# Two folded attentions: the softmax's maximum goes into ScalarE's bias and its sum comes from ScalarE's accumulator

## The reference, cut to what matters

```
h = (x - mean) / sqrt(var + 1e-5)
scores[b, head, s, k] = (h Wq) . (ctx Wk) * 64 ** -0.5      # 32 keys k; a mask, all true
x = x + softmax(scores over k) (ctx Wv) Wo
```

## Time and profile before

| | |
|---|---|
| median of 3 runs | 574.77 us (573.92 to 574.93) |
| profiled execution | 573.43 us, of which the span from the first to the last instruction is 571.6 us |
| TensorE busy | 483.7 us (85%), mean granted clock 0.901 |
| VectorE busy | 325.1 us (57%) |
| ScalarE busy | 238.7 us (42%) |
| GpSimd busy | 241.6 us (42%) |

### The profile page before, as it was taken

How to read it: one execution, slowest core, us unless ns; L and a number is a source line. 1 busy time by engine, 2 the same in 40 slices (tenths; PEclk the granted TensorE clock), 3 DMA queues, 4 the chain that set the end, 5 groups by cost and what they waited for, 6 DMA issues and landing times.

```text
span 571.6 us, 9125 instructions
## 1 busy us (share of the span) xinstructions
PE 483.7 (85%) x3256; PEld 388.0 (68%) x3256; DVE 325.1 (57%) x1137; ACT 238.7 (42%) x473; POOL 241.6 (42%) x350
## 2 busy tenths in 40 slices
PE   2799894779869986995495599999899899999997
PEld 2558383769556625683385399998553788899997
DVE  4866427844996832778751155643776944433334
ACT  2653744324246541444650054421644395334340
POOL 5781866455326011277777525663760340000000
PEclk9799997559758997996599699999999999999999
DMA  9999720311860056800111212114500000000002
GB/s 275 334 205 208 216 99 1 110 34 36 274 193 1 1 147 162 245 1 0 34 51 50 79 57 81 45 34 157 149 2 0 2 2 0 1 1 1 1 1 75
DMA packets 56861, 48.04 MB, mean 84 GB/s; under 512 B 6082, under 2 KB 47240, under 8 KB 56688
## 3 DMA queue, kind: packets, MB, share of 16 engines
q1 hardware_dynamic: 53728, 42.06, 26.5%
q0 software_dynamic: 2656, 4.88, 2.7%
q10 hardware_dynamic: 432, 0.52, 0.4%
HBM read 35.21 MB, written 12.82 MB: 84 GB/s over the span
## 4 chain that ended last, share of the span: by engine, by line
PE 61%; DVE 23%; POOL 6%; issue 5%; ACT 2%; DMA 1%; ACTq 0%; POOLq 0%; DVEq 0%
PE ps L1266 10%; PE ps L1204 7%; DVE st L1660 5%; PE ps L1087 4%; PE ps L1089 4%; PE ps L1088 4%; POOL tok L2381 4%; PE ps L835 3%; PE ps L775 3%; PE ps L722 2%; PE ps L765 2%; DVE mv L1663 2%; PE ps L858 2%; PE ps L838 2%; DVE mx L1698 2%
## 5 line engine op out<-in xcount | busy, mean ns | idle before, releaser
L2113 DVE SCALAR_TENSOR_TENSOR x<-ps,gate,x 128x128 f32<-128x128 f32 x128 | 36.0, 344 | 54.8 <-PE ps L1266 54.8
L1266 PEld LDWEIGHTS ps<-moe_w,big 128*128 128x128 f32 x512 | 61.1, 192 | 3.9 <-issue 1.7
L1538 ACT ACTIVATE big<-ps,col 128x512 f32<-128x512 f32 x64 | 42.2, 689 | 48.2 <-PE ps L1089 48.1
L1266 PE MATMUL ps<-moe_w,big 128*128 128x128 f32 x512 | 61.4, 275 | 0.9 <-DVE x L2102 0.9
L2472 POOL DMA_INDIRECT res<-qT,dest x43 | 42.5, 988 | 40.7 <-DVE qT L2088 25.6
L722 PE MATMUL ps<-con,xn 128*128 128x128 f32 x148 | 28.6, 326 | 28.8 <-ACT xn L1474 15.4
L1530 ACT ACTIVATE big<-ps 128x320 f32<-128x320 f32 x56 | 24.0, 439 | 56.7 <-PE ps L1089 56.6
L722 PEld LDWEIGHTS ps<-con,xn 128*128 128x128 f32 x148 | 19.8, 167 | 39.2 <-DVE xn L1678 35.8
L1204 PE MATMUL ps<-moe_w,big 128*128 128x128 f32 x344 | 41.1, 275 | 0.6 <-ACT big L1530 0.6
L2271 POOL TENSOR_SCALAR rstd<-mv 128x4 f32<-128x4 f32 (+1 forms) x35 | 9.0, 258 | 76.8 <-DVE mv L1663 75.8
L1204 PEld LDWEIGHTS ps<-moe_w,big 128*128 128x128 f32 x344 | 39.8, 192 | 0.8 <-ACT big L1530 0.8
(11 more groups left out here) (353 smaller groups left out, 1179.7 us busy)
## 6 DMA issues: line engine op xcount, KB each, us to landing
ring<-in_ew SPq DMA_DIRECT2D x20, 256.0 KB, 4.8
moe_w<-in_m0w SPq DMA_DIRECT2D x16, 256.0 KB, 6.3
moe_w<-in_m2w SPq DMA_DIRECT2D x16, 256.0 KB, 5.6
tok<-zero SPq DMA_DIRECT2D x1, 2580.0 KB, 27.6
big<-tok SPq DMA_DIRECT2D x7, 322.5 KB, 2.9
res<-zero SPq DMA_DIRECT2D x1, 2048.0 KB, 29.1
moe_w<-in_ew SPq DMA_DIRECT2D x8, 256.0 KB, 5.6
big<-res SPq DMA_DIRECT2D x4, 512.0 KB, 5.0
```

The source lines that it names most:

```text
L1266: last = mm(ps[7 - i % 2 if i >= B else 6 + i % 2][:, cols(c)], big[:, FC * (e % 2) + f, i % B, cols(c)], w[:, e, F + P * f:F + P * f + P] ...
L1538: A(big[:, 2 * (e % 2) + f, t, :], bank[:, :], ACT.Gelu, bias=V("m3b1", 2 * e + f)).then_inc(h_act, 1)
L2113: last = v.scalar_tensor_tensor(out=x[:, C * t + c, :], in0=bank[:, cols(c)], scalar=gate[:, C * t + c, e:e + 1], in1=x[:, C * t + c, :], ...
```

## The change

VectorE no longer subtracts the maximum and no longer sums. It turns each maximum m into -m * rstd with a scalar_tensor_tensor on the maxima alone (in L1 two of these, since its chunks lie in another order than rstd's), and waits for rstd before it. ScalarE's exponential takes this as its bias, exp(rstd * s + (-m * rstd)), and gives the sum over the keys from its accumulator. Bias and sum belong to one head of one chunk, so there is now one exponential per chunk and head: 8 of 128x32 for an L1 tile instead of 4 of 128x64, and 4 of 128x32 for an L2 tile as before. The mask's constant BIG becomes a power of two.

```diff
-BIG = 1e30
+BIG = 2.0 ** 100
...
             def fsoft(name):
-                smax, norm, R = n["smax"], n["norm"], ATT[name]["R"]
+                smax, norm, H = n["smax"], n["norm"], ATT[name]["H"]
 
                 def stage(t):
                     act.wait_ge(s_max[t], smax)
                     act.wait_ge(rstd_ready[t], rstds(t, norm))
                     for q in range(C):
                         c = C * t + chunk_at(name, q)
-                        mine = big[:, 0, t, R * q:R * (q + 1)]
-                        last = A(mine, mine, ACT.Exp, scale=rstd[:, c:c + 1])
+                        for h in range(H):
+                            mine = soft(name, t)[:, q, h, :]
+                            last = A(mine, mine, ACT.Exp, bias=mx[:, C * t + q, h:h + 1], scale=rstd[:, c:c + 1],
+                                     accum_out=rs[:, C * t + q, h:h + 1])
                     last.then_inc(f_exp, 1)
...
             def fscore(name):
                     link(v.tensor_tensor(soft(name, t), s_, mask, ALU.add))
                     link(v.tensor_reduce(top, soft(name, t), AX.X, ALU.max))
-                    v.tensor_tensor(soft(name, t), soft(name, t), bc(top, [P, C, H, NK], [3]), ALU.subtract).then_inc(s_max[t], 1)
+                    dve.wait_ge(rstd_ready[t], rstds(t, norm))
+                    apart = 2 if name == "L1" else 1
+                    for a in range(apart):
+                        m = C // apart
+                        i = v.scalar_tensor_tensor(out=top[:, m * a:m * a + m, :], in0=top[:, m * a:m * a + m, :], scalar=-1.0,
+                                                   in1=bc(rstd[:, C * t + a:C * t + C:apart], [P, m, H], [2]), op0=ALU.mult, op1=ALU.mult)
+                    i.then_inc(s_max[t], 1)
...
             def fsoft(name):
                     total = rs[:, chunks(t), 0:H]
-                    link(v.tensor_reduce(total, soft(name, t), AX.X, ALU.add))
                     link(v.reciprocal(total, total))
```

More of the change, by code:

```diff
@@ L1711, in fscore @@
                 n["smax"] += 1
-                smax, H = n["smax"], ATT[name]["H"]
+                smax, H, norm = n["smax"], ATT[name]["H"], n["norm"]
                 def stage(t):
```

## The result

The median over 8 runs is 578.16 us (573.82 to 579.83), that of before, over 8 runs too, 575.19 us (573.92 to 577.92). The ratio is 1.0050, with a 95% interval of 1.0028 to 1.0072, or 1.6 to 4.1 us. Forecast were 579.6 us (576.0 to 583.0), slower.

What follows compares the result with a forecast made beforehand. VectorE was taken to bound both attention stretches, ScalarE to bound L1 afterwards. L1 +4.6 and L2 +0.2 gave +4.8 us on 574.77, so 579.6 us, range 576.0 to 583.0.

Steps and rivals of the forecast that it cites:

- L1: First attention stretch, about 148 to 165.5 us: exponentials end 5.0 us later, last sum saves 0.4, net +4.6 us.
- L2: Second attention stretch, about 255 to 266 us: VectorE still stalls behind GpSimd's weight splits; 0 to +0.3, taken as +0.2 us.
- Who sets the pace: Attention stretches: VectorE is the bound before; after, ScalarE never stops in L1, from about 154.5 to 168.6 us.
- the prediction's 2.15: Rival that VectorE stays the bound: needs L1 tile exponentials of at most 2.15 us; total 571.6 us; chance 0.05.
- The price per head: ScalarE start-to-start per head and chunk: exponential 0.217, bias pointer 0.09, accumulator read 0.09, together 0.40 us (0.31 to 0.51).
- The block: One L1 tile's eight exponentials with the last read on ScalarE: 3.30 us against 1.06 before.
- read-hidden: Rival: accumulator read fully overlapped on ScalarE, 0.31 us per head, L1 +1.6; total 575.9 to 576.6 us; chance 0.10.
- serial rival: Next accumulating exponential may wait for the read on ScalarE, 0.51 us per head; +7.6 + 0.6, total 583.0 us; chance 0.18.
- VectorE's part: Per L1 tile, subtraction 0.42 and sum 0.41 go, two small instructions at 0.25 come: net -0.58 us on VectorE.
- Nothing later: After the attention stretches: no later wait absorbs the delay, both counted at full weight; the absorbing rival had chance 0.05.
- The added wait for rstd: VectorE's score stage: covered by GpSimd finishing earlier, costs nothing; without cover, a power of 1.04 us paid once.
- My signs to look for: Profile after: reciprocal waits some 1.5 us per tile; wrong if L2 stalls exceed 0.5 us more than twice or TensorE's clock differs.

Runs made afterwards that it cites:

- ladder of four block lengths: Kernel before with L1's exponentials as 8 of 32 columns: scale only 575.25 us; plus bias 575.76; plus accumulator read 576.35; plus both 579.42.
- bias-only kernel: Kernel before with L1's exponentials split by head and given the bias, no accumulator; VectorE sums but does not subtract; 575.76 us, ratio 1.0007.
- bare split: Kernel before with only L1's exponentials split by head, 8 of 128x32 with scale; subtraction and sum stay on VectorE; 575.25 us, ratio 1.0001.
- kernel with L1 alone: The change applied only to the L1 attention, L2 keeping the old lines, against the kernel before; 579.42 us, ratio 1.0073.

## Why the prediction was right

- **Who sets the pace.** Right. Before, VectorE; after, ScalarE without a gap for 13.85 us. The ladder of four block lengths shows ScalarE become the slower of the two between 1.80 and 2.54 us a block; the prediction's 2.15, the longest block with which the change would pay, lies between them.
- **The price per head**, 0.217 + 0.09 + 0.09 = 0.40: measured 0.40, each term by itself (0.21 in the bare split; +0.09 with the bias; +0.09 with the read). The block, 3.30: measured 3.30. The read-hidden and the serial rival are both out by the timeline: the next accumulating exponential starts 0.09 to 0.10 after the read. The Trainium skill's page "ScalarE: Activation LUTs", section "What ACT_TABLE_LOAD costs", gave 2.54 us for the block, which is the bias-only kernel to the hundredth; what it leaves out is the read.
- **VectorE's part.** -0.58 per tile forecast, 16.45 - 14.12 = 2.33 over four tiles measured; the pair of small instructions takes 0.23 (0.25).
- **L1**, +4.6: measured +4.15. The larger part is the walk along ScalarE: blocks and turns from first to last took 13.85 us, not 14.1, since there are six overlaps and not five, the turns took 0.57 and 0.36 in place of 0.60 and 0.38, and the blocks behind the first 3.26 to 3.28. And behind the last block 0.56 fell away in place of 0.4: the sum with its hand-over is 0.45, and the next stage's addition now starts 0.09 before the product has ended, where it had started behind it.
- **L2**, +0.2: measured -0.18. Right in kind: the stall passed on to the small instruction, 1.18 us. Two sizes were off. I had left GpSimd's splits where they stood before, but the one that held the small instruction ended 8.03 us after L2's first mask addition (269.85), where its counterpart before ended after 8.34 (263.41): its rstd ahead of them began 0.13 earlier in the stretch, and its copies and subtractions took 0.61 and 1.27 where before some took 0.73 and 1.32. And from there to L2's end it took 2.2 us, not the 2.3 to 2.4 of the walk; the last product started at 271.86, 0.11 after the last split's end.
- **Nothing later.** Right for the most part. In the kernel with L1 alone the timed runs gave the full 4.2 us (3.0 to 5.4). In the profiles what follows L1's end, L2 left out, is 0.8 us shorter there and 0.9 in the whole change, which is within the scatter of these pieces; 4.15 - 0.18 = 4.0 us lies inside the measured 1.6 to 4.1. That the median is only 3.0 us above before stays open.
- **The sum.** +4.8 forecast, +4.0 in the two stretches, +3.0 by the medians. The terms for L1 and L2 both erred upward, by 0.45 and 0.38 us. The forecast time of 579.6 missed the measured 578.16 by 1.4 us: 1.8 too much for the change, less 0.4 by which before itself now measured higher (575.19 against 574.77). That last part is chance.
- **The added wait for rstd.** Free, as said. But "1.04 us once" as the wait for the case that the cover is gone was too low: it was 2.33 and 3.62 when GpSimd came late, because what counts is how late rstd is, not how long the power takes.
- **My signs to look for.** VectorE's reciprocal waits 1.94, 1.72 and 2.78 us, but only 0.41 in the first tile, where statistics of tile 3 fill the time. One sign of being wrong did come: in L2 three of the small instructions and products took over 0.5 us (0.72, 1.18, 0.56), where I had allowed two. The third was hidden, since VectorE waited 1.09 us for ScalarE behind it. And TensorE's granted clock: 0.73 in L1 before and 0.53 after, 0.50, the lower of its two levels throughout, in both over the 10.24 us behind L1, 0.97 against 0.88 in the 10 us behind that, then 1.00 in both. The piece from L1's end to L2 was no longer for it.

## What to carry to other kernels

An accumulator or a bias per row works per instruction, so with two groups that each need their own, ScalarE's instruction count doubles: on small tiles compare the block (start-to-start distance times count) with the time that the other engine spends on one tile, not the shares of busy time over the kernel. When a max or shift may be shared by several groups, share it and keep wide instructions. A wait moved to the engine that works for all tiles holds up the other tiles' work queued behind it: here 2.33 us of it went with some 0.6 us more of the stretch than a wait on ScalarE.

## What the runs showed of the hardware

On ScalarE a [128, 1] bias and an accumulator read each put 0.09 to 0.10 us between one start and the next, with or without the other, and two accumulating exponentials follow one another without more. A VectorE instruction on four columns with two SBUF inputs took 1.18 us in place of 0.17 under a 128x512 subtraction of GpSimd's, but 0.17 in the middle of GpSimd's 128x4 power of 1.04 us. A 128x128 product with two SBUF inputs took 0.56 in place of 0.29 under GpSimd's copy. Four one-column tensor_scalar with a pointer took 0.58 with and without a split beside them. Four tensor_scalar of 32 columns from SBUF to SBUF took up to 2.45 in place of 0.68, held up by the copy and by the subtraction.
